# A two-layer gated block: probabilities scaled in rows and turned by plain transposes, and four smaller moves around the first layer's FFN

## The reference

```python
def _L0_ffn_ref(hidden_state, w1, b1, w2, b2):
    h = _dyn_quant_linear(hidden_state, w1, b1)      # one scale for the whole tensor,
    h = jax.nn.gelu(h, approximate=False)            # s = max(|x|)/127, x rounded to int8
    return _dyn_quant_linear(h, w2, b2)              # 2048 rows: 512 -> 2048 -> 512

def _L1_xattn_ref(input1, input2, theta_w, ...):     # per batch of 8
    theta_x = jnp.einsum('ld,bdt->btl', theta_w, input2) + theta_b
    phi_x = jnp.einsum('ld,bdt->blt', phi_w, input1) + phi_b[:, None]
    p = jax.nn.softmax(jnp.einsum('btl,bls->bts', theta_x, phi_x), axis=-1)  # 512 x 512
    g_x = jnp.einsum('ld,bdt->btl', g_w, input1) + g_b
    t_x = jnp.einsum('bts,bsl->blt', p, g_x)
    ...                                              # layer norm over (l, t), relu
    return jnp.einsum('ol,blt->bot', out_w, h) + out_b[None, :, None] + input2

x = x + jnp.tanh(g_xattn[0]) * _L0_xattn_ref(ctx, ctx, _layernorm(x), ssm_kernel, D, 8)
x = x + jnp.tanh(g_ffn[0]) * _L0_ffn_ref(_layernorm(x), w1, b1, w2, b2)
x = x + jnp.tanh(g_xattn[1]) * _L1_xattn_ref(_layernorm(x), ctx, ...)
x = x + jnp.tanh(g_ffn[1]) * _L1_ffn_ref(_layernorm(x), ...)
```

## Time and profile before

| what | us |
|---|---|
| median of 3 runs | 661.16 |
| lowest, highest | 660.31, 661.72 |
| the profiled execution, its own time | 661.48 |
| its span in the trace | 659.7 |
| TensorE busy in the span | 626.7 (95%) |
| VectorE, ScalarE, GpSimd busy | 539.5, 486.6, 345.4 |

### The profile page before, as it was taken

The page is one execution under the profiler, slowest core; times in us unless marked ns, Lnnn a source line. Parts: engine busy times, 40 slices in busy tenths (PEclk is TensorE's granted clock), DMA queues, the critical chain, the costliest instruction groups (busy, mean ns, idle before and its releaser), DMA issues.

```text
span 659.7 us, 9713 instructions
## 1 busy us (share of the span) xinstructions
PE 626.7 (95%) x2959; PEld 376.7 (57%) x2989; DVE 539.5 (82%) x1063; ACT 486.6 (74%) x725; POOL 345.4 (52%) x430
## 2 busy tenths in 40 slices
PE   4899999999999899999999999999997999999997
PEld 4677777777776445444446666666533444444443
DVE  2697888889999698966789677777798999999865
ACT  4459784866637898997753476666669999999984
POOL 2389887887872274200001000002388899898951
PEclk9799999999999999999999999999999999999999
DMA  8949896899997345148378900000123665666551
GB/s 302 376 153 305 290 328 209 286 341 338 316 269 283 133 187 196 60 125 329 117 135 170 238 17 16 16 16 0 32 65 119 168 176 159 183 202 172 175 159 49
DMA packets 127862, 118.92 MB, mean 180 GB/s; under 512 B 83456, under 2 KB 90384, under 8 KB 126672
## 3 DMA queue, kind: packets, MB, share of 16 engines
q1 hardware_dynamic: 120384, 104.23, 51.8%
q10 hardware_dynamic: 7440, 14.24, 6.5%
HBM read 68.04 MB, written 30.49 MB: 149 GB/s over the span
## 4 chain that ended last, share of the span: by engine, by line
PE 77%; ACT 8%; DVE 7%; issue 5%; DMA 2%; POOL 1%; SPq 0%; ACTq 0%; POOLq 0%; DVEq 0%
PE ps L1184 21%; PE ps L1474 14%; PE ps L1490 8%; PE ps L1340 6%; PE ps L1299 5%; PE ps L1404 4%; PE ps L1431 4%; PE ps L1400 4%; PE ps L1380 2%; PE ps L1390 2%; ACT turn L970 2%; ACT arena L917 2%; PE ps L1449 2%; PE ps L1193 1%; DMA arena<-kpad_d 1%
## 5 line engine op out<-in xcount | busy, mean ns | idle before, releaser
L1184 PE MATMUL ps<-arena 128*128 128x288 f32 x640 | 163.2, 412 | 6.4 <-DMA arena<-kpad_d 4.0
L1184 PEld LDWEIGHTS ps<-arena 128*128 128x128 f32 x640 | 121.1, 193 | 39.7 <-issue 4.7
L1474 PE MATMUL ps<-arena 128*128 128x512 bf16 x510 | 113.6, 379 | 5.0 <-DVE arena L2061 4.8
L1474 PEld LDWEIGHTS ps<-arena 128*128 128x128 bf16 x512 | 49.5, 98 | 67.0 <-DVE arena L2061 4.6
L683 POOL TENSOR_TENSOR arena<-arena 128x512 f32<-128x512 f32 x64 | 80.3, 1274 | 9.1 <-DVE arena L2061 8.1
L583 POOL TENSOR_TENSOR arena<-arena 128x1024 f32<-128x1024 f32 x32 | 60.6, 1893 | 20.6 <-issue 11.5
L1490 PE MATMUL ps<-arena 128*128 128x512 bf16 x241 | 57.1, 379 | 1.9 <-ACT arena L1084 0.7
L1299 PE MATMUL ps<-arena 128*128 128x512 bf16 (+1 forms) x248 | 56.2, 379 | 0.9 <-ACT arena L917 0.4
L1340 PE MATMUL ps<-arena 128*128 128x512 bf16 x251 | 55.3, 379 | 1.7 <-DVE arena L1828 1.4
L590 POOL TENSOR_TENSOR turn<-turn 128x512 f32<-128x512 f32 x31 | 40.5, 1305 | 22.3 <-DVE turn L1638 22.3
L2061 DVE SCALAR_TENSOR_TENSOR arena<-ps,up_scale,arena 128x512 f32<-128x512 f32 x64 | 46.7, 745 | 5.3 <-ACT arena L1060 4.2
(11 more groups left out here) (229 smaller groups left out, 1300.4 us busy)
## 6 DMA issues: line engine op xcount, KB each, us to landing
arena<-in_L_ffn_w SPq DMA_DIRECT2D x48, 512.0 KB, 6.2
arena<-kpad_d ACTq DMA_DIRECT2D x16, 512.0 KB, 7.2
hq_d<-arena SPq DMA_DIRECT2D x14, 512.0 KB, 2.7
tern_d<-late SPq DMA_DIRECT2D x24, 256.0 KB, 5.4
arena<-in_ctx SPq DMA_DIRECT2D x4, 1024.0 KB, 12.3
arena<-in_x SPq DMA_DIRECT2D x4, 1024.0 KB, 14.8
arena<-in_L_ffn_w ACTq DMA_DIRECT2D x8, 512.0 KB, 5.7
arena<-in_ctx SPq DMA_DIRECT2D x2, 2048.0 KB, 10.3
```

The source lines that it names most:

```text
L1184: last = pe.matmul(ps[:, 4 * s + lo, 0:NB * PAIRS], toep[:, u, (LB - 1 - lo + li) * P:(LB - lo + li) * P], kv[:, s, li, :], start=(li == 0 ...
L1474: last = pe.matmul(ps[:, bank, :], xq4T[:, s, 4 * j + k, :], w[:, k, c * L:(c + 1) * L], start=(k == 0), stop=(k == LB - 1))
```

## The change

Five things change, most of them in several engines' lists:

1. `prob_T` becomes a transpose by the f32 identity, and VectorE multiplies each 128 x 512 row of `prob` by `rrec` in place (`normal_row`) where it wrote a diagonal. In the loop one row is ahead of `latent_beta` and three behind.
2. `w1_widen(3)` leaves VectorE; GpSimd does it, between `norm_x1(1)` and `norm_x1(2)`, behind a `partition_all_reduce` of a constant.
3. `theta(7)` moves ahead of `rows_T(0)`, and `rows_T(0)` and its copy go in two halves with a wait each. On ScalarE `theta_out(5)` moves ahead of `quant_x(0)`, and `theta_out(6)` and `theta_out(7)` ahead of `quant_x(1)`. Counts of `xqb_ready` and `xq_tr` rise by one.
4. Of the fourth part of the hidden rows' first group ScalarE quantises half and VectorE the other half, after the cast of the second part. SyncE's fourth load of `x_res` waits for its cast.
5. The ten unread matmuls go, and the second product waits for `x2_added`, given when bank 2j+1 has been read, and not for `x2_done`.

```diff
@@ GpSimd
             norm_x1(1)
+            po.done(pool.partition_all_reduce(amg[:, 1:2], eps_ln[:, 0:1], P, RED.max))
+            pool.wait_ge(S["o_done"], HEADS + 2)
+            pool.wait_ge(S["w1_in"], 16 * 4)
+            w = fw1T[:, :, 3 * L:4 * L]
+            pool.tensor_scalar(w, w.bitcast(I16), 1.0, 0.0, ALU.mult, ALU.add).then_inc(S["w1_ready"], 1)
             norm_x1(2)
@@ ScalarE
-            for b in range(2, G + 1):
+            for b in range(2, G + 2):
                 theta_out(b)
...
             quant_x(0)
+            for b in range(G + 2, NB):
+                theta_out(b)
             quant_x(1)
-            for b in range(G + 1, NB):
-                theta_out(b)
...
-                    tiles = 4 if k else 2
+                    tiles = 2 if k in (0, 3) else 4
@@ TensorE
-            for b in range(NB - 1):
+            for b in range(NB):
                 theta(b)
...
             def rows_T(g):
-                pe.wait_ge(S["xqb_ready"], g + 1)
...
-                for n in range(16):
-                    last = pe.transpose(dst[:, n * P:(n + 1) * P], wqb[:, g % 2, n * P:(n + 1) * P], identb[:, :])
-                last.then_inc(S["xq_tr"], 1)
+                parts = (range(16),) if g else (range(8, 16), range(8))
+                for m, part in enumerate(parts):
+                    pe.wait_ge(S["xqb_ready"], g + 2 if g else m + 1)
+                    for n in part:
+                        last = pe.transpose(dst[:, n * P:(n + 1) * P], wqb[:, g % 2, n * P:(n + 1) * P], identb[:, :])
+                    last.then_inc(S["xq_tr"], 1)
...
             rows_T(0)
-            theta(NB - 1)
...
-            for n in range(10):
-                pe.matmul(ps[:, 7, :], identb[:, :], fw2T[:, 0, :], start=True, stop=True)
...
-                    pe.wait_ge(S["x2_done"], G * r + j + 1)
+                    pe.wait_ge(S["x2_added"], G * (r - 1) + j + 1)
...
-                return pe.matmul(ps[:, 3 + k, tb * P:(tb + 1) * P], prob[:, p, tb, k * P:(k + 1) * P], diag[:, tb, :],
-                                 start=True, stop=True)
+                return pe.transpose(ps[:, 3 + k, tb * P:(tb + 1) * P], prob[:, p, tb, k * P:(k + 1) * P], identf[:, :])
@@ VectorE
-            w1_widen(3)
             for n in range(NT // 2):
                 largest(n)
...
+                    if (q, c) == (0, 1):
+                        v.wait_ge(S["hq_ready"], 4)
+                        dv.done(v.tensor_scalar(hqi2[:, 1, 2 * L:4 * L].rearrange("p (f n) -> p f n", f=2), hid[:, 0, 14:16, :], isx[:, 1:2], None,
+                                                ALU.mult))
...
-                    dv.done(v.tensor_tensor(tmp2[:, k % 2, :], ps[:, 2 * j + 1, :], tmp2[:, k % 2, :], ALU.add))
+                    v.tensor_tensor(tmp2[:, k % 2, :], ps[:, 2 * j + 1, :], tmp2[:, k % 2, :], ALU.add).then_inc(S["x2_added"], 1)
...
-            def normal_diag(k):
-                v.tensor_scalar(diag[:, k, :], identf[:, :], rrec[:, k:k + 1], None, ALU.mult).then_inc(S["pn_ready"], 1)
+            def normal_row(p, k):
+                v.tensor_scalar(prob[:, p, k, :], prob[:, p, k, :], rrec[:, k:k + 1], None, ALU.mult).then_inc(S["pn_ready"], 1)
```

More of the change, by code:

```diff
@@ L455, in _ @@
                     sp.wait_ge(S["hq_ready"], 3)
+                if g == 3:
+                    sp.wait_ge(S["hq_ready"], 6)
                 sp.dma_start(x_res[:, G * g:G * g + G, :], x1_d[:, G * g:G * g + G, :]).then_inc(rows_in[g], 16)
@@ L940, in _ @@
             gelu(1, 3, range(12))
-            act.wait_ge(S["xq_tr"], NG)
+            act.wait_ge(S["xq_tr"], NG + 1)
             w2_quant(0)
@@ L1370, in _ @@
                     last.then_inc(S["mm2_done"], 1)
-            pe.wait_ge(S["x2_done"], NT + 1)
+            pe.wait_ge(S["x2_added"], NT - 3)
             pe.wait_ge(c_in[0], 32)
@@ L1735, in rows_out @@
             def rows_out(g):
-                v.wait_ge(S["xq_tr"], g + 1)
-                v.tensor_copy(xqT[:, :, g * L:(g + 1) * L].rearrange("p k (t n) -> p t k n", t=G),
-                              bank_bf(4 + 2 * (g % 2), 2).rearrange("p (t k n) -> p t k n", t=G, k=LB)).then_inc(S["xq_out"], 1)
+                for m, tiles in enumerate((slice(0, G),) if g else (slice(2, G), slice(0, 2))):
+                    v.wait_ge(S["xq_tr"], g + 2 if g else m + 1)
+                    last = v.tensor_copy(xqT[:, :, g * L:(g + 1) * L].rearrange("p k (t n) -> p t k n", t=G)[:, tiles],
+                                         bank_bf(4 + 2 * (g % 2), 2).rearrange("p (t k n) -> p t k n", t=G, k=LB)[:, tiles])
+                last.then_inc(S["xq_out"], 1)
             def rows_widen(g):
@@ L1819, in widen_h @@
                         v.wait_ge(S["mm2_done"], G * (q - 1))
+                    if (q, c) == (0, 3):
+                        dv.wait()
                     v.tensor_copy(hq[:, q % 2, 4 * c:4 * c + 4, :].rearrange("p f n -> p (f n)"),
                                   hqi2[:, c % 2, :]).then_inc(S["hq_ready"], 1)
+                    if (q, c) == (0, 1):
+                        v.wait_ge(S["hq_ready"], 4)
+                        dv.done(v.tensor_scalar(hqi2[:, 1, 2 * L:4 * L].rearrange("p (f n) -> p f n", f=2), hid[:, 0, 14:16, :], isx[:, 1:2], None,
+                                                ALU.mult))
             def to_residual(k):
@@ L1857, in _ @@
                     v.wait_ge(S["a_out"], k + 1)
-                    dv.done(v.tensor_tensor(tmp2[:, k % 2, :], ps[:, 2 * j + 1, :], tmp2[:, k % 2, :], ALU.add))
+                    v.tensor_tensor(tmp2[:, k % 2, :], ps[:, 2 * j + 1, :], tmp2[:, k % 2, :], ALU.add).then_inc(S["x2_added"], 1)
                     if j >= 1:
                         to_residual(k - 1)
-                    dv.wait()
+                    v.wait_ge(S["x2_added"], k + 1)
                     dv.done(v.tensor_tensor(tmp2[:, k % 2, :], tmp2[:, k % 2, :], sw2b[:, :], ALU.mult))
@@ L1905, in normalise @@
                     dv.wait()
-                    normal_diag(k)
+                    normal_row(p, k)
             def latent_stats(b):
@@ L1938, in latent_ln, with latent_ln_normalise @@
                 latent_beta(b)
-            def latent_ln_normalise(b):
+            def latent_ln_normalise(b, p):
                 latent_var(b)
@@ L1946, in latent_ln_normalise @@
                 dv.wait()
-                normal_diag(0)
-                normal_diag(1)
+                normal_row(p, 0)
                 latent_beta(b)
-                normal_diag(2)
-                normal_diag(3)
+                for k in range(1, 4):
+                    normal_row(p, k)
             def attn_context(b, ended=False):
@@ L2033, in attn_body @@
                 if nxt2:
-                    latent_ln_normalise(b)
+                    latent_ln_normalise(b, 1 - p)
                 elif nxt:
-                    normalise(b + 1)
+                    normalise(b + 1, 1 - p)
                 if late and b == NB - 2:
@@ L2047, in _ @@
             row_max(0)
-            normalise(0)
+            normalise(0, 0)
             attn_body(0, 0, True, True, False)
```

22 lines of the change are left out of this document (11 added, 11 removed).

## The result

| what | before | after |
|---|---|---|
| median of 6 executions each, us | 660.85 | 656.49 |
| lowest, highest | 660.31, 664.07 | 654.29, 657.74 |
| after / before | | 0.9921 (95%: 0.9894 to 0.9949) |
| the profiled execution: own time, span | 661.48, 659.7 | 657.13, 655.3 |
| busy: TensorE, VectorE, ScalarE, GpSimd | 626.7, 539.5, 486.6, 345.4 | 611.7, 546.4, 483.6, 347.7 |

A forecast was written before the change was run, and what follows sets the result against it. TensorE alone bounds second-layer attention; before the first FFN product the chain passes through four engines. 661.48 + 2.75 - 1.05 - 10.9 - 0.75 = 651.5, less 0.3 for the median: 651.3 us, range 646.5 to 655.5.

The forecast's parts named there:

- GpSimd's insertion: Before the first FFN product: inserted gaps of 6.05 and 6.93 us make `norm_x1(2)` 5.15 us late and `mm1` 2.75 later.
- rival 2: Before the first FFN: TensorE, idle about 3.5 us before `theta(4)`, finds its clock at 1.2 GHz: +2.0, 653.3 us; chance 0.20.
- The upper bound: Start of the first FFN product (`mm1`): at most 4.7 us later, around a forecast of +2.75; lower bound -1.4.
- The rule on GpSimd's loads: GpSimd before the first FFN: each fresh kernel load costs about 6 us, so the first maximum saves the second nothing.
- Turns: Second-layer attention: plain transposes of the probabilities take 1.82 us a batch off TensorE; six batches give -10.9 us.
- Rivals 4 and 5: Attention: plain transposes as dear as products, 663.9 us, chance 0.03; or TensorE's clock falls there, 665.7 us, chance 0.03.
- VectorE's rows: Attention: scaling a row costs VectorE 0.46 us, +0.26 over a diagonal, +1.04 a batch, covered by its idle time.
- Rival 3: Attention: VectorE becomes the bound, at 0.75 us a row: +3.4, 654.7 us; chance 0.07.
- Batch 0: Start of second-layer attention: VectorE's last row sets the first turn, some 1.05 us earlier; bounds -2.7 and 0.
- Second product: Second FFN product: TensorE starts up to 1.3 us earlier without unread matmuls, and group 1's 1.43 us wait goes whole.
- Tail: Last two attention batches to the end: VectorE takes over, what follows moves by -0.75 us; bounds -1.8 and 0.
- rival 1: Before the first FFN: GpSimd's two gaps don't block or are much shorter; -1.4 instead of +2.75, 647.1 us; chance 0.18.

## Why the prediction was wrong, point by point

The gaps of the trace before and those that the insertion added, as stretches (the last but one number is DMA's share); of before:

```profile
214.00:220.00 6.00, 6.00 (x15) 2.47 (x13) 3.48 (x6) 4.69 (x8) 0.01 (x1) 1.00 0.51 190
220.40:227.30 6.90, 4.63 (x29) 2.60 (x31) 5.63 (x9) 5.99 (x6) 0.04 (x1) 1.00 0.26 96
```

and of after:

```profile
199.30:206.40 7.10, 6.67 (x47) 5.47 (x47) 7.03 (x13) 6.12 (x10) 0.00 (x0) 1.00 0.97 364
206.80:216.00 9.20, 9.20 (x40) 5.30 (x38) 5.80 (x17) 1.19 (x2) 0.01 (x1) 1.00 0.60 235
```

- **GpSimd's insertion**: this is the term that failed. The mechanism was right and the size was off: +5.15 us for `norm_x1(2)` and +2.75 for the front in the sum; measured were +8.46 and +7.73. Three pieces make up the 5.0 between them. First, the gaps, 3.3 us (8.46 - 5.15). I priced them with the one gap of each kind in the trace, 6.05 and 6.93, where DMA's share was 0.51 and 0.26, and put them where it is 0.97 and 0.60. There the second gap was 9.20 to 9.63 in four profiles, the first 5.57 to 7.13; that DMA makes the difference is likely and not shown. Second, the clock, 1.2 us in this pair of profiles: the sum had nothing for it and left it to rival 2. From `norm_x1(2)` to the turns of the first rows I had 226.3 - 213.5 = 12.8, which is what the kernel with the filled idle time took (12.86); the changed kernel took 14.02. Third, turns and copies, 0.5 us: 1.9 in the sum, 2.41 between 231.88 and 234.29. The kernel without the insertion has the same 2.4, so this is not GpSimd's; 0.2 of it is the missing first record, which the 225.50 of the earlier trace rows lacks as well.
- **The upper bound** of that term, +4.7, came from waiting order alone. It held neither a longer gap nor a slower clock together with one, and rival 2 was priced with the short gaps. Two causes that make each other worse (a longer wait, and a clock that falls in it) belonged in one case at the top of the range.
- **The rule on GpSimd's loads** was used rightly: the first maximum saved the second nothing. In the changed kernel the real maximum cannot show it: its data came at 227.31 + 0.17 = 227.48, when the 6 us behind its MODIFY_POOL_CONFIG at 221.5 were just over, and it ran at 227.61. The kernel with more maxima shows it, 9.98 and then 6.01 us for the same change of direction.
- **Turns**: -10.9 forecast, -10.72 measured; sixteen turns 1.75 us, batch 14.41. Rivals 4 and 5 did not occur.
- **VectorE's rows**: 0.46 forecast, 0.40 measured, +0.20 each over a diagonal. Its idle time in a batch fell from 3.81 us to 1.19, that is by 1.82 + 4 x 0.20 = 2.62, where 2.86 was forecast. Rival 3 did not occur in the loop.
- **Batch 0**: the step was right that rows and not TensorE set the first turns.

```profile
367.83 0.49 DVE L1911 TENSOR_SCALAR arena<-arena,rrec 128x512 f32<-128x512 f32 x1
```

```profile
368.37 1.97 PE L1410 MATMUL ps<-identf,arena 128*128 128x128 f32 x16 [1.33 <-DVE arena L1911]
```

  TensorE waited 1.33 us for the last row (it had been forecast to wait 1.6), and the stretch gave 1.42 where 1.05 was expected; cheaper rows are most of that.
- **Second product**: group 1 goes without a stop, as forecast. This answers to the earlier trace rows:

```profile
300.54 3.61 PE L1348 MATMUL ps<-arena 128*128 128x512 bf16 x16 [1.62 <-DVE arena L1814]
...
304.64 51.96 PE L1348 MATMUL ps<-arena 128*128 128x512 bf16 x235
```

  From the first FFN product to here it is 66.25 us against 67.41, the forecast 1.3 within 0.14. What I had priced at nothing is what the ten matmuls did for the clock. It is up to 1.5 us of TensorE's work in some executions, and 0.6 to 0.8 us at batch 0's turns; in this profile it is nothing (3.61 us).
- **Tail**: -0.75 forecast, -1.05 measured, and VectorE runs through, as said: its statistics of batch 6 start at once, where the earlier trace rows had 1.16 us of idle time.

```profile
460.28 0.70 DVE L1922 BATCH_NORM_STATS2 bn<-ps 128x6 f32<-128x512 f32 x1
```

- **Without the insertion** the prediction's sum was 647.1 (its rival 1, for another reason). Measured were 648.8 and 648.4, and 646.6 with six unread matmuls back: the terms other than the front hold to within 1.7 us together.

## What to carry to other kernels

A `partition_all_reduce` among ordinary GpSimd operations cost two gaps here, 5.6 to 10.6 us in and 6.8 to 11.5 us back, paid anew each time. Before one is put into an idle time, add both, at the longest length seen, and look at what stands behind it on the queue. Matmuls that nobody reads can be holding TensorE's clock: price their removal in the granted clock of the work behind them, and price any new wait of TensorE with the slower work that can follow it.

## What the runs showed of the hardware that I had not expected

- GpSimd's gap into a `partition_all_reduce` was 5.55 to 6.1 us, and 6.8 to 7.7 us back, where DMA's share was 0.55 or less; beside a busier one they reached 10.6 and 11.5 in one and the same kernel. But the gap in was 5.57 and 5.74 beside shares of 1.04 and 1.03, and the gap back 7.07 beside 0.70, so something else has a part; I have not found it.
- The same stretch of instructions, with the same idle times of 0.87 and 1.62 us ahead of the second product, found TensorE's clock at 1.00 in some executions and at 0.50 in others. The Trainium skill (TensorE: Matmul & The Clock Gate, Part 1: The HAM clock gate) says that the clock has two levels and that how many matmuls run at the lower one at a kernel's start varies from run to run; the rows show such a variation in the middle of a program, with 3.61 and 5.12 us for the same sixteen matmuls.
- A tensor_scalar of 128 x 512 on on-chip operands costs VectorE 0.40 us in a row of single ones, against 0.20 for one of 128 x 128.
